# An attention-and-FFN kernel: pair 1's second FFN layer behind x and scores of pair 3, w2's passes spread

## The reference, cut to what matters

```python
x = x + xattn(layernorm(x), ctx)         # 8 heads, 77 context rows, softmax
# FFN on the result:
h = layernorm(x) * ln_gamma + ln_beta
w1 = (fc1_q - 128) * fc1_scales          # 256 x 1024, by groups of 128 rows
y = silu(h @ w1 + fc1_bias)
w2 = (fc2_q - 128) * fc2_scales          # 1024 x 256
x = x + 0.5 * (y @ w2 + fc2_bias)
```

## Time and profile before

| | us |
|---|---|
| median of 3 runs | 189.15 |
| lowest, highest | 188.84, 191.03 |
| the profiled execution, whole | 188.6 |
| its span, first to last instruction | 186.8 |
| PE busy | 180.7 (97%) |
| DVE busy | 122.4 (66%) |
| ACT busy | 122.5 (66%) |
| POOL busy | 116.2 (62%) |

### The profile page before, as it was taken

How to read it: one execution, slowest core, us unless ns; L and a number is a source line. 1 busy time by engine, 2 the same in 40 slices (tenths; PEclk the granted TensorE clock), 3 DMA queues, 4 the chain that set the end, 5 groups by cost and what they waited for, 6 DMA issues and landing times.

```text
span 186.8 us, 3886 instructions
## 1 busy us (share of the span) xinstructions
PE 180.7 (97%) x1502; PEld 177.0 (95%) x1502; DVE 122.4 (66%) x261; ACT 122.5 (66%) x230; POOL 116.2 (62%) x159
## 2 busy tenths in 40 slices
PE   7999899899899999999999999999999999999994
PEld 7999699689899999999999999999999999999994
DVE  0287988899969464964496557937594768255341
ACT  3287880599918981898368944896289817962580
POOL 5032998569983977099707972597439762776220
PEclk9999999999999999999999999999999999999999
DMA  6997990000000100010001000100001000100101
GB/s 171 325 399 185 357 353 13 2 0 4 2 0 0 60 0 0 4 56 0 4 0 56 4 0 0 33 30 0 0 4 56 0 4 0 56 4 0 56 4 56
DMA packets 9480, 10.72 MB, mean 57 GB/s; under 512 B 2268, under 2 KB 8183, under 8 KB 9335
## 3 DMA queue, kind: packets, MB, share of 16 engines
q1 hardware_dynamic: 8837, 9.70, 15.7%
q10 hardware_dynamic: 626, 0.79, 1.5%
HBM read 8.38 MB, written 2.10 MB: 56 GB/s over the span
## 4 chain that ended last, share of the span: by engine, by line
PE 78%; DVE 9%; POOL 9%; ACT 1%; issue 1%
PE T L852 22%; PE H L838 21%; PE T L823 11%; PE S L802 11%; PE S L809 4%; PE S L755 3%; POOL q_sb L316 3%; POOL w_lo L321 3%; PE S L733 2%; DVE w_lo L631 2%; POOL probs L279 1%; DVE q_sb L625 1%; PE T L740 1%; PE H L740 1%; POOL rstd L290 1%
## 5 line engine op out<-in xcount | busy, mean ns | idle before, releaser
L311 POOL TENSOR_TENSOR y_lo<-y,y_hi 128x512 fp32r<-128x512 f32 x28 | 37.6, 1363 | 2.1 <-ACT y_hi L434 1.6
L279 POOL TENSOR_TENSOR probs<-probs,rsum 128x616 f32<-128x616 f32 x16 | 19.1, 1218 | 31.4 <-DVE rsum L583 31.4
L852 PE MATMUL T<-w_hi,y_hi 128*128 128x256 f32 x128 | 36.7, 286 | 0.6 <-DVE x_sb L594 0.6
L838 PE MATMUL H<-hT_hi,w_hi 128*128 128x256 f32 x128 | 36.7, 287 | 0.1
L838 PE MATMUL H<-hT_lo,w_hi 128*128 128x256 f32 x128 | 35.5, 277 | 0.0
L838 PE MATMUL H<-hT_hi,w_lo 128*128 128x256 f32 x128 | 35.5, 277 | 0.0
L852 PE MATMUL T<-w_lo,y_hi 128*128 128x256 f32 x128 | 35.5, 277 | 0.0
L852 PE MATMUL T<-w_hi,y_lo 128*128 128x256 f32 x128 | 35.4, 277 | 0.0
L430 ACT ACTIVATE y<-H,vec 128x256 f32<-128x256 f32 x64 | 26.5, 467 | 6.6 <-PE H L838 6.6
L403 ACT ACTIVATE probs<-probs,rstd 128x616 f32<-128x616 f32 x16 | 12.9, 807 | 27.1 <-DVE probs L571 27.1
L588 DVE TENSOR_TENSOR pT_lo<-S,pT_hi 128x640 fp32r<-128x640 f32 x16 | 13.1, 823 | 18.1 <-ACT pT_hi L407 18.1
(11 more groups left out here) (127 smaller groups left out, 460.6 us busy)
## 6 DMA issues: line engine op xcount, KB each, us to landing
q_sb<-in_L_ffn_fc_q SPq DMA_DIRECT2D x2, 1024.0 KB, 8.0
out_x<-x_sb SPq DMA_DIRECT2D x16, 128.0 KB, 1.8
x_sb<-in_x SPq DMA_DIRECT2D x7, 256.0 KB, 8.2
s_sb<-in_L_ffn_fc_scales SPq DMA_DIRECT2D x2, 512.0 KB, 12.0
s_sb<-in_L_ffn_fc_scales SPq DMA_DIRECT2D x1, 1024.0 KB, 7.7
wq_sb<-in_L_xattn_Wq SPq DMA_DIRECT2D x1, 512.0 KB, 5.6
wo_sb<-in_L_xattn_Wo SPq DMA_DIRECT2D x1, 512.0 KB, 8.1
wk_sb<-in_L_xattn_Wk ACTq DMA_DIRECT2D x1, 384.0 KB, 4.1
```

What stands on the lines that cost most here:

```text
L279: nc.gpsimd.tensor_tensor(p, p, rsum[:, j, :].unsqueeze(2).to_broadcast([P, HEADS, J]), ALU.mult).then_inc(norm_done, 1)
L311: nc.gpsimd.tensor_tensor(y_lo[:, two, :], y[:, two, :], f32(y_hi[:, two, :]), ALU.subtract).then_inc(y_lo_done, 1)
L838: ins = mm(r[:, q * W:(q + 1) * W], wt[:, c, m * P:(m + 1) * P], ht[:, c, :], start=c == q == i == 0, stop=c == q == 1 and i == 2)
L852: ins = mm(o, yt[:, m, j * P:(j + 1) * P], wt[:, m, :], start=m == 0 and i == 0, stop=m == M - 1 and i == 2)
```

## The change

Nothing is computed differently; instructions are put in another order on all four engines, between pair 1's probabilities and pair 2's scores. On PE the third block of the first layer goes between the two probability transposes, x's transposes of pair 2 go ahead of the attention output of pair 1, and `fc2(0, 0)` goes behind both scores of pair 2. The list of banks changes with it; each bank is filled by the same names in the same order as before.

```diff
@@ PE
                 prob_transposes(1, 0)
+                fc1(0, 2)
                 prob_transposes(1, 1)
-                fc1(0, 2)
                 fc1(0, 3)
+                x_transposes(2)
                 attention_out(1, 0)
                 attention_out(1, 1)
-                x_transposes(2)
-                fc2(0, 0)
                 for a in range(2, LAST):
                     scores(a, 0)
                     scores(a, 1)
+                    if a == 2:
+                        fc2(0, 0)
@@ DVE
                 vw_lo_part(1, 2)
-                stats1(2)
                 dve.wait_ge(q2_in, 16)
                 dve.wait_ge(s2_in, 16)
                 dequantize_w2(0)
+                prob_lo(1, 0)
                 dequantize_w2(1)
-                prob_lo(1, 0)
                 prob_lo(1, 1)
+                stats1(2)
+                x_lo(2)
                 lower_w2(0)
-                lower_w2(1)
                 add_attention(1, 0)
                 add_attention(1, 1)
-                x_lo(2)
+                lower_w2(1)
+                shift_scores(2, 0)
                 make_hn(1)
@@ ACT
                 hidden(0, 0)
+                prob_hi(1, 0)
                 hidden(0, 1)
-                prob_hi(1, 0)
                 prob_hi(1, 1)
-                for n in range(2):
-                    half = slice(n * M // 2, (n + 1) * M // 2)
-                    act.wait_ge(w2_done, n + 1)
-                    nc.scalar.activation(w2_hi[:, half, :], w2_sb[:, half, :], ACT.Copy).then_inc(w2_hi_done, 1)
+                x_hi(2)
+                w2_hi_part(0)
                 hidden(0, 2)
+                w2_hi_part(1)
                 hidden(0, 3)
-                nc.scalar.activation(table_probe[:, :], neg_half[:, 0:1], ACT.Exp)
-                x_hi(2)
                 residual(0)
+                nc.scalar.activation(table_probe[:, 0:1], neg_half[:, 0:1], ACT.Exp)
@@ POOL
+                normalize(1, 0)
+                normalize(1, 1)
+                lower_y(0, 0)
+                lower_y(0, 1)
+                rsqrt1(2)
+                lower_y(0, 2)
+                root2(1, 0)
+                root2(1, 1)
+                lower_y(0, 3)
+                residual_roots(1)
+                add_b2(0)
```

More of the change, by code:

```diff
@@ L67, in build_program @@
         if a > 1:
-            order += [(f"S{a}.0", "S0"), (f"S{a}.1", "S1"), (f"F2.{a - 2}.1", "T1"), (f"HT{a - 1}", "S0")]
+            order += [(f"S{a}.0", "S0"), (f"S{a}.1", "S1")] + [("F2.0.0", "T0")] * (a == 2) + [(f"F2.{a - 2}.1", "T1"), (f"HT{a - 1}", "S0")]
         order += [(f"F1.{a - 1}.{p}", f"H{1 - p % 2}") for p in range(HP)]
         order += [(f"PT{a}.0", "S1"), (f"PT{a}.1", "S0"), (f"AO{a}.0", "T0"), (f"AO{a}.1", "T1")]
-        order += [(f"XT{a + 1}", "S1")] * (a < LAST) + [(f"F2.{a - 1}.0", "T0")]
+        order += [(f"XT{a + 1}", "S1")] * (a < LAST) + [(f"F2.{a - 1}.0", "T0")] * (a > 1)
     order += [(f"F2.{LAST - 1}.1", "T1"), (f"HT{LAST}", "S0")] + [(f"F1.{LAST}.{p}", f"H{1 - p % 2}") for p in range(HP)]
@@ L125, in build_program @@
         neg_half = small("neg_half", [P, NT])
-        table_probe = small("table_probe", [P, 1])
+        table_probe = small("table_probe", [P, 2])
         bn1, mv1 = small("bn1", [P, NT, 6]), small("mv1", [P, NT, 2])
@@ L280, in normalize, with root2, residual_roots @@
                                             ALU.mult).then_inc(norm_done, 1)
-                def rsqrt2(a):
+                def root2(a, j):
                     o = a % 2
[L285 to L291, removed]
+                    pool.wait_ge(mv2_done, a * UT + j + 1)
+                    nc.gpsimd.tensor_scalar(vars2[:, o, 1, j:j + 1], mv2[:, o, j, 1:2], 1.0 + EPS, EPS * EPS,
+                                            ALU.mult, ALU.add).then_inc(vars2_done, 1)
+                    pool.wait_ge(vars2_done, a * 3 + j + 1)
+                    nc.gpsimd.tensor_tensor(rstd2[:, o, 1, j:j + 1], vars2[:, o, 1, j:j + 1], neg_half[:, 0:1],
+                                            ALU.pow).then_inc(rstd2_done, 1)
+                def residual_roots(a):
+                    o = a % 2
                     nc.gpsimd.tensor_scalar(vars2[:, o, 0, :], mv2[:, o, :, 1], EPS, None, ALU.add).then_inc(vars2_done, 1)
@@ L334, in _ @@
                 rsqrt1(1)
-                rsqrt2(0)
+                root2(0, 0)
+                root2(0, 1)
+                residual_roots(0)
                 pool.wait_ge(b2_done, 1)
-                for a in range(1, NA):
+                normalize(1, 0)
[9 more added lines that the diff above has]
+                add_b2(0)
+                for a in range(2, NA):
                     normalize(a, 0)
@@ L343, in _ @@
                         lower_y(a - 1, p)
-                    rsqrt2(a)
+                    root2(a, 0)
+                    root2(a, 1)
+                    residual_roots(a)
                     if a == LAST:
@@ L434, in hidden, with w2_hi_part @@
                     nc.scalar.activation(y_hi[:, two, :], y[:, two, :], ACT.Copy).then_inc(y_hi_done, 1)
+                def w2_hi_part(n):
+                    half = slice(n * M // 2, (n + 1) * M // 2)
+                    act.wait_ge(w2_done, n + 1)
+                    nc.scalar.activation(w2_hi[:, half, :], w2_sb[:, half, :], ACT.Copy).then_inc(w2_hi_done, 1)
                 def shift_w1(n):
@@ L484, in _ @@
                 vw_hi_part(1, 2)
-                nc.scalar.activation(table_probe[:, :], neg_half[:, 0:1], ACT.Silu)
+                nc.scalar.activation(table_probe[:, 1:2], neg_half[:, 0:1], ACT.Silu)
                 hidden(0, 0)
+                prob_hi(1, 0)
                 hidden(0, 1)
-                prob_hi(1, 0)
                 prob_hi(1, 1)
-                for n in range(2):
-                    half = slice(n * M // 2, (n + 1) * M // 2)
-                    act.wait_ge(w2_done, n + 1)
-                    nc.scalar.activation(w2_hi[:, half, :], w2_sb[:, half, :], ACT.Copy).then_inc(w2_hi_done, 1)
+                x_hi(2)
+                w2_hi_part(0)
                 hidden(0, 2)
+                w2_hi_part(1)
                 hidden(0, 3)
-                nc.scalar.activation(table_probe[:, :], neg_half[:, 0:1], ACT.Exp)
-                x_hi(2)
                 residual(0)
+                nc.scalar.activation(table_probe[:, 0:1], neg_half[:, 0:1], ACT.Exp)
                 for a in range(2, NA):
@@ L682, in _ @@
                 dequantize_w2(0)
+                prob_lo(1, 0)
                 dequantize_w2(1)
-                prob_lo(1, 0)
                 prob_lo(1, 1)
+                stats1(2)
+                x_lo(2)
                 lower_w2(0)
-                lower_w2(1)
                 add_attention(1, 0)
                 add_attention(1, 1)
-                x_lo(2)
+                lower_w2(1)
+                shift_scores(2, 0)
                 make_hn(1)
                 for a in range(2, NA):
-                    shift_scores(a, 0)
+                    if a > 2:
+                        shift_scores(a, 0)
                     score_maxima(a, 1)
```

## The result

The changed kernel takes 187.26 us (median of 4 runs, 187.12 to 187.59) against 189.0 for the kernel before (4 runs, 188.67 to 191.03): a ratio of 0.990, 95% interval 0.985 to 0.994. It is about 1% faster: the interval leaves out 1, and the difference stays under 2%. The gain is more than was forecast, and 187.26 lies just outside the range given (187.4 to 189.5). Two later comparisons on other occasions gave 0.988 (0.983 to 0.994) and 0.989 (0.984 to 0.994).

What follows compares the result with a forecast made beforehand. PE's idle time was taken as the bound: 1.43 us from two gaps less 0.55 of new stalls gives a gain of 0.9, so 189.15 - 0.9 = 188.2 us median; range 187.4 to 189.5, main case chance 0.60.

Steps and rivals of the forecast that it cites:

- The bound: PE: its time ahead of 58.4 us reaches the end unchanged; re-ordering can give back at most 1.43 us of idle time.
- rivals 2 and 3: `lower_y(0, 2)` gets ahead of `lower_w2(0)`, 189.4, chance 0.13; gain given back at `split_h(1)` or `normalize(2, 0)`, 189.0 to 189.2, chance 0.12.
- rival 1: L625 and `normalize` don't meet on DVE and POOL, no new stall: 1.43 us gained, 187.7, chance 0.15.
- The first gap: PE between pair 1's two probability transposes, released by POOL's `normalize`: 0.63 us lost, closed by `fc1(0, 2)`.
- the second: PE between pair 2's x transposes and `fc2(0, 0)`, released by DVE's L594: 0.80 us lost, closed by the new order.
- The stall in `fc2(0, 0)`: PE wants POOL's `lower_y(0, 3)` at 52.9 and has it at 53.4: a new stall of 0.5 us.
- 0.05 at hn: PE's `fc2` and first block of tile 1 end at 54.4, hn is there at 54.3 to 54.4: another 0.05 us.
- that root: POOL's `rsqrt1(2)`, running to 47.05: DVE's `lower_w2(0)`, issued at 46.6, waits for it and ends at 48.2.
- The long passes: DVE and POOL take turns by whole instructions; charges: w_lo 1.13, L625 1.15, y_lo 1.25 us, the later issued waiting.
- The base: The median of three runs stands 0.55 us above the profiled execution, so the median forecast starts from 189.15.

Runs made afterwards that it cites:

- `gap1_only`: The kernel before with only `fc1(0, 2)` between pair 1's probability transposes on PE and `prob_hi(1, 0)` ahead of `hidden(0, 1)` on ACT: 188.9 us, ratio to before 0.996.
- `root_away`: The changed kernel with POOL's `rsqrt1(2)` moved behind `lower_y(0, 3)`, so POOL is idle when `lower_w2(0)` is issued: 188.29 us, ratio to before 0.996.
- `long_ahead`: The changed kernel with POOL's `lower_y(0, 1)` done a second time, to be running when DVE issues `lower_w2(0)`: 189.38 us, ratio to before 1.003.
- `late_y3`: The changed kernel with POOL's `lower_y(0, 3)` done twice and only the second counted for PE: 188.87 us, ratio to before 1.000.
- `stats_back`: The changed kernel with `stats1(2)` alone put back ahead of `dequantize_w2(0)` on DVE: 187.8 us, ratio to before 0.995.

## Why the prediction was right or wrong

**The bound, right.** PE's idle time is all there was to win, and nothing behind `fc1(1, 0)` gave it back but 0.14 us. No wait of L594, no wait at the scores, none at pair 2's probability transposes: rivals 2 and 3 did not happen, rival 1's time (a gain of 1.43, profile 187.2) came out at 187.12.

**The first gap, right in place, wrong in worth.** The prediction added 0.63 for it to 0.80 for the second. `gap1_only` shows that it was worth 0.0 by itself: the two were one wait for DVE's list, seen at two places. Since the change closed both, the sum was not hurt.

**The size of the gaps, low by 0.19.** d fell by 1.62 where the idle times were put at 1.43. Start to start, the transposes cost 0.47 to 0.52 for five and 0.35 for four (43.65 to 44.00); the prediction took 0.55 and 0.44 from the chain's row. That is 0.12 of the 0.19; the other 0.07 is net of small changes between rows, among them `fc2(0, 0)`, 2.72 instead of the 2.86 that it took behind its wait. Behind the stretch 0.14 were lost again.

**The stall in `fc2(0, 0)`, the step that failed.** The prediction put it at 0.5, and 0.05 at hn. It was 0. The step is "`lower_w2(0)` is issued at 46.6, waits for that root, and ends 48.2". It was issued at 46.48, did not wait, took 1.22 and ended at 47.70; `root_away` gives the same 1.22 without a root. With the adds behind it, y_lo came at 52.74, not 53.35. Of these 0.61 us, 0.5 is that step. The other 0.1 is a slip: by the charge of 1.25 that the working names, a y_lo begun at 52.0 ends at 53.25. (A second slip, the first y_lo from 42.0 to 43.1 instead of 43.25, goes the other way.) The long passes were priced well: the first L645 1.92 (1.95 in the working), w_lo against a y_lo 2.02 in `long_ahead`. The Trainium skill (SBUF — State Buffer, "SBUF: two separate sides" and "Who interferes with whom") has it that a GpSimd instruction that reads SBUF and is issued first keeps VectorE's pass with two SBUF inputs out for its whole length. For `normalize` and y_lo the traces agree (1.92, 2.02), for the two-element root they do not (1.22 either way), and the measurement decides. Why the root does not hold the pass is open; no run varies its size or its operation, and spans on POOL are rough in the profile.

**Rival 1 came out for another reason than its own.** It supposed that L645 and `normalize` don't meet. They did, for about 0.7 us (1.92 against the 1.21 that each of the two in the earlier trace rows takes), as in the main working.

**The chances.** I gave 0.60 to a stall and 0.15 to none, on a margin that even by my own working was 0.5 wide and that rested on the smallest instructions in the sum, whose behaviour no row that I had picked showed. The trace of the kernel before has a hint that I overlooked:

```profile
L625 DVE SCALAR_TENSOR_TENSOR q_sb<-q_sb,s_sb x2: 1211/1214/1218, 41.1 to 42.3; 128x1024 f32<-128x1024 int32 x2
```

The second of these passes is issued at 42.3, while POOL's veps, held since 41.30, is still to end at 42.42. By turns of whole instructions it would have had to wait some 0.1 us for the veps; both passes take 1.21 to 1.22. `late_y3` and the changed kernel's own times (52.74 against 52.92) show that the outcome turned on 0.1 us. The two cases deserved nearly equal chances.

**The base.** 0.94 us lie between the forecast median and the measured one. 0.55 are the stall; 0.05 the gaps with their loss behind; the other 0.34 is the base. I carried over the 0.55 by which the median of three stood above its profiled execution; for the changed kernel it is 0.14. Since the start moves single executions by 2 us (36.82 to 38.96 up to `fc1(0, 0)`), a median of three says little at this size.

## What to carry to other kernels

When two engines share a resource by turns, list which instructions take turns in which direction and of what length before summing; a small instruction may be held and not hold. Two idle times on the bound engine can be one wait for the same late list: close one alone and see whether the other grows. A re-ordering like this is one edit on four engines: PE's move of `fc2(0, 0)` alone, and everything but that move, were each over 2 us slower in d than the kernel before (2.26 and 2.43).

## What the runs showed of the hardware

- **A small instruction was held and did not hold.** A one-column vars of POOL, normally 0.19, took 1.00 us beside a w_lo (49.85 above). A two-column root, 0.71 in the changed kernel, took 1.55 in the kernel before, where it was issued behind the second L625 (42.3 to 43.5); in the changed kernel such a root in flight did not lengthen a w_lo that started 0.10 us into it (1.22, and 1.22 in `root_away`).

```profile
42.50 1.55 POOL L274 TENSOR_TENSOR rstd<-veps,neg_half 128x2 f32<-128x2 f32 x1
```

- **A cast with one SBUF input takes turns too.** The cast of hT takes 0.28 to 0.29 us free, and 1.00 when issued at 55.17 behind an `add_b2` that ran from 54.73 to 56.02. The prediction let only the two-input remainder behind it wait.
- **Matmuls of the first layer have two pitches.** 24 of them take 2.72 us in most pairs and 2.83 in the changed kernel's pair 1 (2.79 and 2.80 when it was run again), whose operand was ready only some 0.15 us ahead (at 56.63 for 56.79), with the granted clock at 1.00 in both. Releasing the operand 0.7 us earlier brought 2.72 at that place and 2.83 at the next pair, and `root_away` and `stats_back` have one 2.83 each at a later pair (from 117.15 and 120.62). The cause is open.
- **PE ran at about half its pace near the start of some executions, with a granted clock of 1.00 in the rows.** The sixteen matmuls of L762 took 2.18 us in one execution of the changed kernel and 4.05 in another. The cause is open.
